# Moving the quantisation of one token tile behind the next tile's activation quantisation

## What is computed

```python
def act_quant(x):
    scale = 127.0 / jnp.clip(jnp.max(jnp.abs(x), axis=-1, keepdims=True), 1e-05)
    return jnp.clip(jnp.round(x * scale), -128, 127) / scale
# weights are quantised to -1, 0, 1 times one scale
h = bit_linear(x, w1)            # 1024 -> 4096, on act_quant(x)
h = depthwise_conv1d(h, conv_w, conv_b)   # 3 taps along the tokens
h = silu(h)
return bit_linear(h, w2)         # 4096 -> 1024, on act_quant(h)
x = x + layernorm(ffn(layernorm(x)))
```

## Time and profile before

| what | value |
|---|---|
| median of 16 runs | 9326.09 us (9315.12 to 9348.64) |
| the profiled execution, its own time | 9320.38 us |
| its span on the slowest core (core 7) | 9318.8 us |
| spans of the 8 cores | 9260.5 to 9318.8 us |
| PE busy | 2903.9 us (31%) |
| DVE busy | 3390.5 us (36%) |
| ACT busy | 1064.8 us (11%) |
| POOL busy | 510.5 us (5%) |
| loop over `fi` | about 5000 to 8240 us of the span |

### The profile page before, as it was taken

One profiled execution on the slowest core, in us unless ns is written; L12 is line 12 of the kernel. 1 busy time (PEld: TensorE's weight loads), 2 busy tenths in 40 slices (PEclk: granted clock), 3 DMA queues, 4 the chain that ended last, 5 costly groups with the idle time before them and its releaser, 6 DMA issues.

```text
span 9318.8 us, 47605 instructions; the slowest of 8 cores (9260.5 to 9318.8 us)
## 1 busy us (share of the span) xinstructions
PE 2903.9 (31%) x12144; PEld 1436.4 (15%) x12144; DVE 3390.5 (36%) x6255; ACT 1064.8 (11%) x2053; POOL 510.5 (5%) x604
## 2 busy tenths in 40 slices
PE   3545454111457735444132120101102010103464
PEld 1121312000123333222010010101001010101121
DVE  0111011100112212333344757566574756654212
ACT  0111111001100011000100121111112111120000
POOL 0000000111000000000000111020110101100000
PEclk9955555555568855666555665656556565655686
DMA  1010100000001211111210000000000000031111
GB/s 31 28 42 32 43 27 34 30 23 26 30 31 40 39 44 26 32 32 32 85 45 28 5 12 14 8 12 5 12 5 12 15 8 12 1 108 45 52 47 60
DMA packets 170576, 283.16 MB, mean 30 GB/s; under 512 B 60305, under 2 KB 122987, under 8 KB 165893
## 3 DMA queue, kind: packets, MB, share of 16 engines
q1 hardware_dynamic: 157640, 246.56, 8.8%
q0 software_dynamic: 12672, 33.57, 1.2%
HBM read 223.21 MB, written 55.10 MB: 30 GB/s over the span
## 4 chain that ended last, share of the span: by engine, by line
DVE 34%; PE 27%; DMA 15%; issue 11%; ACT 6%; SPq 3%; DVEq 1%; POOL 1%; ACTq 0%; POOLq 0%
PE ps L243 21%; DVE a_xh_f L264 6%; PE ps L246 6%; DVE a_xh_f L260 4%; ACT a_st L272 3%; DMA a_st<-s_logat 3%; DVE a_xh_f L252 3%; SPq L82 2%; DMA s_wlo<-a_wr 2%; DMA s_rows<-t_tiny 2%; DVE a_w_f L252 2%; DVE a_st L264 2%; DVE a_w L249 2%; DVE a_xl_f L264 2%; DVE a_xtm L252 1%
## 5 line engine op out<-in xcount | busy, mean ns | idle before, releaser
L243 PE MATMUL ps<-a_st,c_o1f 128*1 128x256 f32 (+3 forms) x992 | 412.7, 530 | 1228.8 <-ACT a_st L272 1181.3
L264 DVE SCALAR_TENSOR_TENSOR a_xh_f<-a_xh_f 128x1024 f32<-128x1024 f32 x448 | 583.5, 1303 | 46.6
L243 PE MATMUL ps<-a_xtm_b,a_w 128*128 128x258 bf16 x2048 | 288.3, 285 | 616.4 <-DVE a_xtm_b L264 446.9
L243 PE MATMUL ps<-a_xh,a_w 128*128 128x512 bf16 (+2 forms) x1664 | 390.1, 398 | 244.1 <-DMA a_xh<-s_hq 67.1
L246 PE MATMUL ps<-c_id,a_big 128*128 128x128 f32 x208 | 92.8, 446 | 1164.4 <-DVE a_big L252 530.8
L246 PE MATMUL ps<-c_id,a_xh_f 128*128 128x128 f32 (+1 forms) x536 | 238.2, 444 | 660.0 <-DVE a_xh_f L252 391.6
L252 DVE TENSOR_TENSOR a_xl<-ps,a_xh 128x256 bf16<-128x256 f32 (+1 forms) x264 | 110.0, 416 | 858.0 <-ACT a_xh L272 858.0
L252 POOL TENSOR_TENSOR a_xh_f<-a_xl_f,t_bt 128x256 f32<-128x256 f32 x224 | 259.4, 1186 | 1990.4 <-DMA t_bt<-s_rows 1373.3
L260 DVE TENSOR_SCALAR a_xh_f<-a_xh_f 128x1024 f32<-128x1024 f32 x448 | 345.6, 771 | 47.6
L243 PE MATMUL ps<-t_bt,a_st 128*128 128x16 f32 x1024 | 228.2, 373 | 322.3 <-ACT a_st L272 322.3
L243 PEld LDWEIGHTS ps<-a_xtm_b,a_w 128*128 128x128 bf16 x2048 | 190.3, 101 | 714.7 <-issue 685.8
(11 more groups left out here) (190 smaller groups left out, 4832.1 us busy)
## 6 DMA issues: line engine op xcount, KB each, us to landing
a_st<-s_logat SPq DMA_DIRECT2D x64, 512.0 KB, 3.9
a_xh_f<-w SPq DMA_DIRECT2D x64, 512.0 KB, 3.9
a_xh_f<-w SPq DMA_DIRECT2D x16, 2048.0 KB, 8.1
a_xtm<-xp SPq DMA_DIRECT2D x48, 512.0 KB, 4.8
s_hq<-a_big_b POOLq DMA_DIRECT2D x64, 256.0 KB, 3.8
a_xh<-s_hq SPq DMA_DIRECT2D x128, 128.0 KB, 3.3
a_st<-s_x SPq DMA_DIRECT2D x64, 129.0 KB, 3.2
a_xtm<-xo SPq DMA_DIRECT2D x16, 512.0 KB, 4.8
```

The costliest lines, as they stand in the source:

```text
L243: e.matmul(o, l, r, start=s1, stop=s2), after=after)
L264: e.scalar_tensor_tensor(o, x, s, y, op0=p0, op1=p1), after=after)
```

## The change

Step 6 is split in two functions and is no longer written at the end of its own tile.

- `emit_hq_gps` is written at the very top of the next turn of the loop, ahead of that tile's statistics. It holds POOL's `ug` for groups 0 and 1, and all of group 7: `raws` on POOL, the `Abs` chains on ACT, and the five ending operations on DVE, for both halves.
- `emit_hq_vec` is written in the next tile behind `flb` and `hm`, ahead of its first `h_e`. It holds DVE's work on groups 0 to 6, POOL's `ug` for groups 2 to 6, and the 8 spills.
- After the last turn both follow directly, one behind the other.
- `uts` now go to `xhf[:, 2064:4128]` in place of `sb_big`, and no longer wait for spills. They are made in two halves: `fla` waits for the first four pairs, `flb` for the other four.
- Some waits are added for buffers that are now shared between tiles: on `bk2`, on the first `c1s`, and on the first maximum of `tr2`.

The diff, cut to its core:

```diff
+    def emit_ug(gq, pa, hbk2, htr2l, extra):
...
+    def emit_hq_gps(hbk2, htr2l):
+        nonlocal hq_act, last_raw
+        dvq = [gq for gq in range(KH // 4) if gq not in ACTGQ]
+        ug_map = []
+        for i, gq in enumerate(dvq[:2]):
+            pa = i % 2
+            uo, ug = emit_ug(gq, pa, hbk2, htr2l, hq_par[pa][-1:])
+            ug_map.append((gq, pa, uo, ug))
+        act_fin = {}
+        for gq in ACTGQ:
+            fls = []
+            for hh in range(2):
+                raws = []
+                for j in range(2):
...
+                last_raw = raws[-1:]
+                hq_act = floor_tri_act(
...
+    def emit_hq_vec(hfi, ug_map, act_fin, hbk2, htr2l):
...
+        for i in range(len(dvq)):
+            gq, pa, uo, ug = ug_map[i]
+            w1b = vts(xhf[:, uo:uo + 1024], xhf[:, uo:uo + 1024],
+                      127.5, None, ALU.add, after=ug)
+            fl = floor_sub(bigb[:, gq * 1024:gq * 1024 + 1024],
...
+            ni = i + 2
+            if ni < len(dvq):
+                uo2, ug2 = emit_ug(dvq[ni], pa, hbk2, htr2l, fl[-1:])
...
+        for gq, ftok in hq_fl:
+            sp = P.dma(capd(s_hq, gq * 4 * 128 * TOWN + hfi * 256,
...
     for fi in range(8):
         to = fi * 256
+        if pend_src is not None:
+            pend = ((pend_src[0],) + emit_hq_gps(pend_src[1], pend_src[2])
+                    + (pend_src[1], pend_src[2]))
+            pend_src = None
...
-        for k in range(KD):
-            usl = bigf[:, k * 258:k * 258 + 258]
+        for k in range(4):
+            usl = xhf[:, 2064 + k * 258:2064 + k * 258 + 258]
...
-                      after=[bck] + uts[-1:] + prev_spill, eng="gpsimd")
+                      after=[bck] + uts[-1:], eng="gpsimd")
...
+        fla = floor_sub(xtmb[:, 0:1032], xhf[:, 2064:3096],
+                        xhf[:, 0:1032], sb_st2.ap()[:, 0:1032], uts)
+        uts2 = list(uts)
+        for k in range(4, KD):
...
+        flb = floor_sub(xtmb[:, 1032:2064], xhf[:, 3096:4128],
+                        xhf[:, 0:1032], sb_st2.ap()[:, 0:1032],
+                        uts2[4:] + fla[-1:])
...
+        if pend is not None:
+            emit_hq_vec(*pend)
+            pend = None
         h_e = []
...
-        bk2 = bcast_read(sb_bt.ap()[:, 0:256], R_K2, to, 256, after=[rk2, rr2])
+        bk2 = bcast_read(sb_bt.ap()[:, 0:256], R_K2, to, 256,
+                         after=[rk2, rr2] + hq_g[-1:] + last_raw)
+        pend_src = (fi, bk2, tr2[-1:])
...
+    if pend_src is not None:
+        pend = ((pend_src[0],) + emit_hq_gps(pend_src[1], pend_src[2])
+                + (pend_src[1], pend_src[2]))
+        emit_hq_vec(*pend)
```

More of the change, by code:

```diff
@@ L1049, in build_program @@
     ACTGQ = (7,)
-    prev_aspill = []
+    prev_aspill, prev_dspill, last_raw = [], [], []
     xtmf = sb_xtm.ap()
-    prev_uts, prev_rr2, prev_he, prev_spill = [], [], [], []
+    def emit_ug(gq, pa, hbk2, htr2l, extra):
+        uo = 4128 + pa * 1024
+        ug = []
+        for j in range(4):
+            mh = gq * 4 + j
+            ug.append(vtt(xhf[:, uo + j * 256:uo + j * 256 + 256],
+                          xlf[:, mh * 256:mh * 256 + 256],
+                          sb_bt.ap()[:, 0:256], ALU.mult,
+                          after=[hbk2] + hq_g[-1:] + extra + htr2l,
+                          eng="gpsimd"))
+        hq_g.append(ug[-1])
+        return uo, ug
@@ new lines, in emit_hq_gps @@
+    def emit_hq_gps(hbk2, htr2l):
[12 more added lines that the diff above has]
+                for j in range(2):
+                    mh = gq * 4 + hh * 2 + j
+                    raws.append(vtt(xtmf[:, 1040 + j * 256:1040 + j * 256 + 256],
+                                    xlf[:, mh * 256:mh * 256 + 256],
+                                    sb_bt.ap()[:, 0:256], ALU.mult,
+                                    after=[hbk2] + hq_act[-1:] + htr2l,
+                                    eng="gpsimd"))
+                last_raw = raws[-1:]
+                hq_act = floor_tri_act(
+                    bigb[:, gq * 1024 + hh * 512:gq * 1024 + hh * 512 + 512],
+                    xtmf[:, 1040:1552],
+                    sb_st2.ap()[:, 1040:1552], sb_st2.ap()[:, 1552:2064], raws)
+                fls += hq_act
+            act_fin[gq] = fls[-1]
+        return ug_map, act_fin
@@ new lines, in emit_hq_vec @@
+    def emit_hq_vec(hfi, ug_map, act_fin, hbk2, htr2l):
+        nonlocal prev_aspill, prev_dspill
+        dvq = [gq for gq in range(KH // 4) if gq not in ACTGQ]
+        ug_map = list(ug_map)
+        hq_fl = []
+        for i in range(len(dvq)):
[3 more added lines that the diff above has]
+            fl = floor_sub(bigb[:, gq * 1024:gq * 1024 + 1024],
+                           xhf[:, uo:uo + 1024],
+                           xhf[:, 6176:7200], xhf[:, 7200:8224], [w1b])
+            hq_par[pa] = [fl[-1]]
+            hq_fl.append((gq, fl[-1]))
+            ni = i + 2
+            if ni < len(dvq):
+                uo2, ug2 = emit_ug(dvq[ni], pa, hbk2, htr2l, fl[-1:])
+                ug_map.append((dvq[ni], pa, uo2, ug2))
+        for gq in ACTGQ:
+            hq_fl.append((gq, act_fin[gq]))
+        for gq, ftok in hq_fl:
+            sp = P.dma(capd(s_hq, gq * 4 * 128 * TOWN + hfi * 256,
+                            [[TOWN, 128], [128 * TOWN, 4], [1, 256]]),
+                       bigb[:, gq * 1024:gq * 1024 + 1024], after=[ftok],
+                       eng="gpsimd",
+                       tag=(f"hqa{gq % 2}" if gq in ACTGQ else f"hq{gq % 2}"))
+            if gq in ACTGQ:
+                prev_aspill = [sp]
+            else:
+                hq_d.append(sp)
+            hqs.append(sp)
+        prev_dspill = hq_d[-2:]
@@ L1053, in build_program @@
+    prev_uts, prev_rr2, prev_he = [], [], []
+    pend, pend_src = None, None
     for fi in range(8):
         to = fi * 256
+        if pend_src is not None:
+            pend = ((pend_src[0],) + emit_hq_gps(pend_src[1], pend_src[2])
+                    + (pend_src[1], pend_src[2]))
+            pend_src = None
         dep = ph6b + prev_uts[-1:]
@@ L1121, in build_program @@
         uts = []
-        for k in range(KD):
-            usl = bigf[:, k * 258:k * 258 + 258]
+        for k in range(4):
+            usl = xhf[:, 2064 + k * 258:2064 + k * 258 + 258]
             v1_ = vtt(usl, sb_st.ap()[:, k * 258:k * 258 + 258],
                       sb_abc.ap()[:, 0:258], ALU.mult,
-                      after=[bck] + uts[-1:] + prev_spill, eng="gpsimd")
+                      after=[bck] + uts[-1:], eng="gpsimd")
             uts.append(vtt(usl, usl, sb_bbc.ap()[:, 0:258], ALU.add,
                            after=[v1_, bcl], eng="gpsimd"))
[L1129 to L1132, removed]
+        fla = floor_sub(xtmb[:, 0:1032], xhf[:, 2064:3096],
+                        xhf[:, 0:1032], sb_st2.ap()[:, 0:1032], uts)
+        uts2 = list(uts)
+        for k in range(4, KD):
+            usl = xhf[:, 3096 + (k - 4) * 258:3096 + (k - 4) * 258 + 258]
+            v1_ = vtt(usl, sb_st.ap()[:, k * 258:k * 258 + 258],
+                      sb_abc.ap()[:, 0:258], ALU.mult,
+                      after=uts2[-1:], eng="gpsimd")
+            uts2.append(vtt(usl, usl, sb_bbc.ap()[:, 0:258], ALU.add,
+                            after=[v1_], eng="gpsimd"))
+        flb = floor_sub(xtmb[:, 1032:2064], xhf[:, 3096:4128],
+                        xhf[:, 0:1032], sb_st2.ap()[:, 0:1032],
+                        uts2[4:] + fla[-1:])
         xqs = [flb[-1]]
+        uts = uts2
         bcr = bcast_read(xtmf[:, 1552:1810], R_R1, to, 258, after=[wrr])
@@ L1156, in build_program @@
             c1s.append(act(csl, xhf[:, mh * 258: mh * 258 + 256], AF.Copy,
-                           scale=sb_cw.ap()[:, mh * 3:mh * 3 + 1], after=[h_e[mh]]))
+                           scale=sb_cw.ap()[:, mh * 3:mh * 3 + 1],
+                           after=[h_e[mh]]
+                           + (hq_g[-1:] + last_raw if mh == 0 else [])))
         for mh in range(KH):
@@ L1175, in build_program @@
                      after=h2s + tr2[-2:]
-                     + (prev_aspill + hq_act[-1:] if j == 0 else []))
+                     + (prev_aspill + prev_dspill + hq_act[-1:] if j == 0 else []))
             m2 = vtt(xtmf[:, 1296:1552], a_, b_, ALU.min, after=[m1])
@@ L1255, in build_program @@
-        prev_uts, prev_rr2 = uts[-1:], [rr2]
-        prev_he, prev_spill = h_e[-4:], hq_d[-2:]
+        bk2 = bcast_read(sb_bt.ap()[:, 0:256], R_K2, to, 256,
+                         after=[rk2, rr2] + hq_g[-1:] + last_raw)
+        pend_src = (fi, bk2, tr2[-1:])
+        prev_uts, prev_rr2 = uts[-1:], [rr2]
+        prev_he = h_e[-4:]
+    if pend_src is not None:
+        pend = ((pend_src[0],) + emit_hq_gps(pend_src[1], pend_src[2])
+                + (pend_src[1], pend_src[2]))
+        emit_hq_vec(*pend)
```

## The result

The changed kernel takes 9433.25 us (median of 8 runs, 9403.9 to 9442.67), against 9325.53 us for the kernel before (44 runs). The ratio is 1.011, with a 95% interval of 1.0101 to 1.012: slower by 108 us. The prediction was +95 us, 9421, with 9391 to 9460 as its range. The profiled execution took 9429.81 us by itself; its slowest core is core 0, with a span of 9428.3 us.

A forecast was written before the change was run, and what follows sets the result against it. Waits in sequence, with no engine busy over 36%, were taken to bound the kernel. +132.9 + 0.75 - 31.6 - 7 = +95 us on 9320.4 gives 9415, as a median 9421 us; range 9391 to 9460.

The forecast's parts named there:

- Parts 1 and 2: Per tile, group 7 ahead of the statistics (40.74 us) and seven groups behind `flb` (139.44), against 163.57 before: +16.61 us.
- Part 3: `uts` in halves: `fla` starts 6.61 us earlier, POOL beside it costs 2.66; gain 3.95 us a tile, -31.6 us.
- The rival by which POOL holds DVE for its whole length: While `uts` run beside `fla`, POOL operations cost DVE 5.5 instead of 2.66 us; 9444 us, chance 0.10.
- Part 4: Hidden matmuls during the seven groups: PE does one block ahead, not four, saving 1.0 us a tile, -7 us.
- Part 5: Five or six spills issued while DVE rounds: taken as 0, other bound 2.0 us a tile, +16 us.
- The two faster rivals: `Abs` chains hide under the statistics: 9164 us, chance 0.04; PE runs four banks ahead at `h_e`: 9380 us, chance 0.03.

## Why the prediction was right

It forecast +95 us and +108 were measured. By its own steps, against the means of 56 tiles:

- **Parts 1 and 2**, group 7 ahead of the statistics and the groups behind `flb`: +16.61 us predicted. Measured 40.91 + 139.68 - 163.55 = +17.04. The 0.4 us more are 0.17 between T0 and the squares and 0.24 in the groups. Group 7 put back removed the loss, and both chains hidden turned it into a gain with groups and spills where the change had put them: the cause is shown, not only argued.
- **Part 3**, `uts` in halves: -3.95 predicted, -6.49 + 2.52 = -3.97 measured. With 2.52 / 8 = 0.32 us for each POOL operation, the price held for blocks of 258 too. The rival by which POOL holds DVE for its whole length (5.5 us a tile) fell: 2.52 us were measured. It was the rule of the page "SBUF — State Buffer" of the Trainium skill, section "Who interferes with whom", by which the engine that comes second is blocked for the whole instruction of the first. This trace does not agree: DVE loses 0.32 us for a POOL operation that takes 0.64 to 0.73 us alone.
- **Part 4**, the head start: -1.0 predicted, -0.97 measured. The size was right partly by luck. I took it from one tile with two slow blocks (over 1.06 us), and let two be slow behind the groups too. Over the 56 tiles it is 2.9 in the mean before (two to five in a tile) and 3.2 behind the groups in the changed kernel (two to nine). Both are about one more than I had, and so the difference holds.
- **Part 5**, spills beside DVE: taken as 0, bound 2.0 us. Group 5, in which POOL issues five of them, takes 20.61 us in the mean against 20.30 for groups 2 to 4, so they cost about 0.3 us a tile. Two compares (L260) get longer, the subtracts (L264) stay at 1.23 us:

```profile
5914.31 3.84 POOL L82 DMA_DIRECT2D s_hq<-a_big_b  x5
...
5915.56 0.81 DVE L260 TENSOR_SCALAR a_xh_f<-a_xh_f 128x1024 f32<-128x1024 f32 x1
5916.47 1.23 DVE L264 SCALAR_TENSOR_TENSOR a_xh_f<-a_xh_f 128x1024 f32<-128x1024 f32 x1
5917.80 0.86 DVE L260 TENSOR_SCALAR a_xh_f<-a_xh_f 128x1024 f32<-128x1024 f32 x1
```

- **The term that was missing** is +0.35 us between the last `h_e` and T0, which I had as unchanged. It is 77.06 to 77.27 us in the runs that have the seven groups behind `hm`, and 76.94 and 77.10 in the two that have not. That is no clean split, and its cause stays open.

Over the loop, from first `uts` to last spill, the mean of the eight cores goes from 3169.5 to 3273.2 us, +103.8 where the sum had +95. By tiles: -1.8 in the first (-3.95 predicted), 7 x 12.47 = 87.3 in tiles 2 to 8 (7 x 11.7 = 82), and 18.3 behind the last T0 (17.4). The other 4 us of the medians' difference lie outside the loop, in code that the change leaves alone: the first `uts` starts between 5001 and 5068 us on the cores of the kernel before, and between 5006 and 5067 in the changed kernel.

The two faster rivals fell by the same rows: the squares followed on the `Abs` chain, and PE did one block ahead. Each needed an edit that the change does not have. With it the chains did hide, at about the time that the rival gave (ratio 0.985; its 9164 us are 0.983). PE did run four blocks ahead, but the rival's price was off both ways. The head start itself is worth 2.95 us a tile, not 6.9, since blocks back to back come every 0.89 us. The wait that must go for it, however, holds every block and not only the first four: without it a tile of the changed kernel takes 386.6 us instead of 414.7, 28 us less.

## What to carry to other kernels

In a kernel whose engines run their lists as written, moving work under another stage's waits paid here only where each engine that it touches would have waited anyway, so it has to be written at such a place in every list. The change put 18 `Abs` and five DVE operations, twice, ahead of the steps they were to run beside, and laid open a chain of some 14 us that had been covered. The same operations, written behind the square root and beside `fla` and `flb`, left 3.3 us open behind `hm` and added 0.6 us in `fla` and `flb`. Before moving work into idle time, write down for each engine what stands in front of its next critical operation. And look at which token a wait names: waiting for the newest eviction instead of the one of the own bank cost 26 us a tile, twice what the whole change lost.

## What the runs showed of the hardware

- A POOL operation beside DVE's rounding lengthens one DVE operation by 0.25 to 0.34 us, whether that takes 0.70 or 1.23 us alone, while the POOL operation goes from 0.64 to 0.73 us to between 0.91 and 1.72 us. Five spills issued by POOL in a row (3.84 us) lengthen two compares of DVE, by 0.12 and 0.17 us, and no subtract (1.23 us).
- Out of the same 56 us of idleness PE does two to five of the first blocks of eight matmuls slowly (up to 1.88 us against 1.05), tile by tile, in the kernel before. In the changed kernel the granted clock was 0.50 of full speed, its lower level of 1.2 GHz, through the 139 us of the groups, 0.52 in the 10 us behind them and 1.00 after.
- Blocks of eight 128x258 matmuls come every 0.89 us when PE does not wait, less than the 1.05 us from start to end of a block that stands alone.
